# The first cross attention's 160 keys as 128 + 32 in place of 80 + 80, and a weight centring moved from GpSimd to VectorE in pieces

## What is computed

```python
q = (layernorm(x) @ Wq + bq)      # 16 batches, 64 queries, 16 heads of 16
k = (ctx_1024 @ Wk + bk)          # 1024 keys, most of them masked
v = (ctx_1024 @ Wv + bv)
scores = where(mask, q @ k.T / 4, -1e9)
x = x + softmax(scores) @ v @ Wo + bo
...
q = layernorm_per_head(layernorm(x) @ L0_attn_Wq.T)   # 16 heads of 64; k likewise
```

## Time and profile before

| | |
|---|---|
| time before, median of 3 runs | 843.26 us (841.45 to 844.18) |
| span of the profiled execution | 844.3 us; no separate time is given for it |
| PE / PEld busy | 684.7 us (81%) / 525.9 us (62%) |
| DVE / ACT / POOL busy | 421.2 / 328.4 / 144.2 us |
| iterations b = 1 to 15 of the first cross attention | 44.36 to 201.14 us |

### The profile page before, as it was taken

The page is one execution under the profiler, slowest core; times in us unless marked ns, Lnnn a source line. Parts: engine busy times, 40 slices in busy tenths (PEclk is TensorE's granted clock), DMA queues, the critical chain, the costliest instruction groups (busy, mean ns, idle before and its releaser), DMA issues. The chain is left out here.

```text
span 844.3 us, 18960 instructions
## 1 busy us (share of the span) xinstructions
PE 684.7 (81%) x7638; PEld 525.9 (62%) x7638; DVE 421.2 (50%) x907; ACT 328.4 (39%) x881; POOL 144.2 (17%) x213
## 2 busy tenths in 40 slices
PE   3778887789899999995787689989986764278996
PEld 2556665565456666663665546579985643178995
DVE  5436787764545445514587275836657344011111
ACT  1235444443445544442577363331224141132332
POOL 1011112201100000003334232091000211211121
PEclk9879998999999999995889699989998965598999
DMA  6920000001900000004000000000000009791110
GB/s 174 357 65 2 2 2 1 1 1 34 230 2 2 1 2 1 2 1 127 2 2 3 1 0 2 2 2 2 0 2 2 0 4 318 274 368 39 46 51 23
DMA packets 33161, 45.30 MB, mean 54 GB/s; under 512 B 7998, under 2 KB 26175, under 8 KB 32960
## 3 DMA queue, kind: packets, MB, share of 16 engines
q1 hardware_dynamic: 28672, 33.31, 12.3%
q0 software_dynamic: 2256, 7.37, 2.7%
q10 hardware_dynamic: 2160, 3.60, 1.6%
HBM read 36.91 MB, written 7.89 MB: 53 GB/s over the span
## 5 line engine op out<-in xcount | busy, mean ns | idle before, releaser
L393 ACT ACTIVATE a_pr<-a_bank,a_nms 128x160 f32<-128x160 f32 x128 | 49.1, 391 | 59.4 <-DVE a_nms L723 57.0
L859 PE MATMUL a_bank<-ident,a_pr 128*80 128x128 f32 x256 | 41.5, 289 | 25.7 <-DVE a_pt L699 23.2
L2101 ACT ACTIVATE f_hb<-f_bank,cols 128x128 f32<-128x128 f32 x96 | 35.2, 367 | 63.1 <-PE f_bank L2219 58.2
L859 PEld LDWEIGHTS a_bank<-ident,a_pr 128*80 128x80 f32 x256 | 26.1, 124 | 46.3 <-ACT a_pr L393 31.8
L2219 PE MATMUL f_bank<-f_xts,f_w 128*128 x384 | 51.6, 293 | 0.8 <-DVE f_xts L2171 0.8
L2219 PEld LDWEIGHTS f_bank<-f_xts,f_w 128*128 128x128 f32 x384 | 50.2, 208 | 1.7 <-issue 1.2
L629 DVE TENSOR_REDUCE a_negmx<-a_bank 128x2 f32<-128x320 f32 x64 | 30.4, 475 | 33.6 <-PE a_bank L851 33.6
L699 DVE COPY a_pt<-a_bank 80x512 f32<-80x512 f32 x60 | 40.9, 682 | 10.5 <-PE a_bank L859 9.8
L2229 PE MATMUL f_bank<-f_w,f_hb 128*128 128x256 f32 x192 | 44.0, 383 | 0.0
L2229 PEld LDWEIGHTS f_bank<-f_w,f_hb 128*128 128x128 f32 x192 | 36.2, 194 | 4.5
L358 POOL TENSOR_TENSOR a_spr<-a_linv,a_hm 128x128 f32<-128x128 f32 x32 | 12.1, 400 | 148.9 <-DVE a_linv L678 136.3
(11 more groups left out here) (361 smaller groups left out, 1607.2 us busy)
## 6 DMA issues: line engine op xcount, KB each, us to landing
f_w<-in_f_w SPq DMA_DIRECT2D x16, 1024.0 KB, 9.8
slots<-a_zero POOLq DMA_DIRECT2D x1, 4112.0 KB, 18.7
f_xs<-slots ACTq DMA_DIRECT2D x13, 257.0 KB, 2.7
...
rows<-in_rows SPq DMA_DIRECT2D x1, 2120.0 KB, 10.1
...
```

The source lines that it names most:

```text
L393: i = act.activation(pr[:, p, j, k, :], s_bank[j][:, k * KW:(k + 1) * KW], ACT.Exp, bias=nms[:, p, j, k:k + 1], accum_out=rsum[:, p, 2 * j ...
L859: m = pe.transpose(dst[0:HK, (2 * k + a) * P:(2 * k + a + 1) * P], pr[:, p, j, k, a * HK:(a + 1) * HK], c.ident[:, :])
L2101: act.activation(hb[:, m, :], bank[m % 4][:, 0:P], ACT.Gelu, bias=c.col("f_b1", e * FC + m)).then_inc(z["act"], 1)
```

## The change

Keys 0 to 127 of the window are now one full part, and keys 128 to 159 a tail. Values: one product of 128 keys, and the tail's values in four column tiles of 32 so that the tail of j lies on partitions 32 j (`tail_values`, L846). Turns: three per batch in place of four: turn 0 (j = 0, 1) and turn 1 (j = 2, 3) of four transposes each, and turn 2 with the tails of all j, eight products with the identity in tiles of 32 columns (L873); they are copied as 512, 512 and 256 columns. Weigh: for each k, four products over the 128 keys (L881) and four over the 32 in tiles of 32 x 32 (L885). The tail values stand behind turn 1, and turn 2 stands behind keys. The centring is in eight pieces (four per weight), each a sum, a scaling and an addition over 512 elements on DVE, at the end of iterations 6 to 13; making the weights `wt` binary moves from iteration 10 to 14. At the start, the product behind `actq` goes to `k_bank`, DVE reads it before the second half of its statistics, and PE waits for it before the keys, not before the queries.

The core of the diff, with the general loop's part left out:

```diff
@@ -196,9 +196,9 @@
-        vs = sb("vs", [HK, 2, 2, D])
+        vs = sb("vs", [P, 2, D + S])
...
-        pt = sb("pt", [HK, 4, 512])
+        pt = sb("pt", [P, 2 * KW // 32, P])
@@ -373,12 +373,6 @@
             for b in range(NT + 1, B):
-                if b in (10, 12):
-                    i, wx = (b - 10) // 2, (bwq, bwk)[(b - 10) // 2]
-                    pool.wait_ge(U["wmean"], i + 1)
-                    tv = wx[:, :, :].rearrange("p k (h n) -> p (k h) n", n=DA)
-                    pool.tensor_tensor(tv, tv, wm[:, i, :].unsqueeze(2).to_broadcast([P, KC * HA, DA]),
-                                       ALU.add).then_inc(U["wcent"], 1)
                 spread(b)
...
@@ -603,18 +597,18 @@

+            dve.wait_ge(z["actp"], 1)
+            dve.tensor_scalar(actq[:, :], k_bank[:, 0:S], HD ** -0.5, None, ALU.mult).then_inc(z["actq"], 1)
+            dve.wait_ge(s_ident, 64)
+            dve.wait_ge(z["actq"], 1)
+            for e in range(2):
+                dve.tensor_scalar(acte[:, e, :], actq[:, :], c.eo[:, e:e + 1], None, ALU.mult).then_inc(z["acte"], 1)
             dve.wait_ge(s_x[1], 16)
...
                 normed(A0, xn, t, 2)
-            dve.wait_ge(z["actp"], 1)
-            dve.tensor_scalar(actq[:, :], o_bank[:, 0:S], HD ** -0.5, None, ALU.mult).then_inc(z["actq"], 1)
-            dve.wait_ge(s_ident, 64)
-            dve.wait_ge(z["actq"], 1)
-            for e in range(2):
-                dve.tensor_scalar(acte[:, e, :], actq[:, :], c.eo[:, e:e + 1], None, ALU.mult).then_inc(z["acte"], 1)
             dve.wait_ge(z["acte"], 2)
@@ -624,6 +618,10 @@
                         ).then_inc(z[f"qbd{e}"], 1)
+
+            def turned_out(g, src, done):
+                a, n = 4 * g, 4 if g < 2 else 2
+                dve.tensor_copy(pt[:, a:a + n, :].rearrange("p a n -> p (a n)"), src[:, 0:n * P]).then_inc(done, 1)

...
@@ -694,9 +692,9 @@
-            def turned(b, j):
-                dve.wait_ge(T["tp"], 4 * (b - 1) + j + 1)
-                dve.tensor_copy(pt[:, j, :], t_bank[0:HK, :]).then_inc(T["pt"], 1)
+            def turned(b, g):
+                dve.wait_ge(T["tp"], 3 * (b - 1) + g + 1)
+                turned_out(g, t_bank, T["pt"])
@@ -705,20 +703,22 @@
-            def center(i):
-
-                if i == 0:
-                    dve.wait_ge(s_bw, 64)
-                dve.reduce_sum(wm[:, i, :], (bwq, bwk)[i][:, :, :].rearrange("p k (h n) -> p (k h) n", n=DA), AXX).then_inc(U["wsum"], 1)
-                dve.wait_ge(U["wsum"], i + 1)
-                dve.tensor_scalar(wm[:, i, :], wm[:, i, :], -1.0 / DA, None, ALU.mult).then_inc(U["wmean"], 1)
+            def center(i, part):
+                n = 4 * i + part
+                wp = (bwq, bwk)[i][:, :, :].rearrange("p k (h n) -> p (k h) n", n=DA)[:, 8 * part:8 * part + 8, :]
+                mp = wm[:, i, 8 * part:8 * part + 8]
+                dve.reduce_sum(mp, wp, AXX).then_inc(U["wsum"], 1)
+                dve.wait_ge(U["wsum"], n + 1)
+                dve.tensor_scalar(mp, mp, -1.0 / DA, None, ALU.mult).then_inc(U["wmean"], 1)
+                dve.wait_ge(U["wmean"], n + 1)
+                dve.tensor_tensor(wp, wp, mp.unsqueeze(2).to_broadcast([P, 8, DA]), ALU.add).then_inc(U["wcent"], 1)
...
-                    if b > 1 and j:
-                        turned(b - 1, j - 1)
+                    if b > 1 and j % 2:
+                        turned(b - 1, j // 2)
@@ -726,22 +726,24 @@
-                    turned(b - 1, 3)
+                    turned(b - 1, 2)
...
-                if b in (6, 8):
-                    center((b - 6) // 2)
-                if b == 10:
+                if 5 < b < 14:
+                    if b == 6:
+                        dve.wait_ge(s_bw, 64)
+                    center((b - 6) // 4, (b - 6) % 4)
+                if b == 14:
...
-            for j in range(4):
-                turned(B - 1, j)
-                if j == 0:
+            for g in range(3):
+                turned(B - 1, g)
+                if g == 0:
@@ -809,7 +811,7 @@
             pe.wait_ge(z["const"], CONST_ANYB)
-            pe.matmul(o_bank[:, 0:S], anyb[0:S, :], c.ident[0:S, 0:S], start=True, stop=True).then_inc(z["actp"], 1)
+            pe.matmul(k_bank[:, 0:S], anyb[0:S, :], c.ident[0:S, 0:S], start=True, stop=True).then_inc(z["actp"], 1)

@@ -834,11 +836,17 @@
-            def values(src, a):
+            def values(src):
...
-                    m = pe.matmul(v_bank[0:HK, a * D:(a + 1) * D], src[:, kk, a * HK:(a + 1) * HK], wv[:, kk, :],
-                                  start=(kk == 0), stop=(kk == KC - 1))
-                return m
+                    pe.matmul(v_bank[:, 0:D], src[:, kk, 0:KM], wv[:, kk, :], start=(kk == 0), stop=(kk == KC - 1))
+
+            def tail_values(src, done):
+                for kk in range(KC):
+                    for j in range(4):
+                        m = pe.matmul(v_bank[32 * j:32 * j + 32, D:D + S], src[:, kk, KM:KW],
+                                      wv[:, kk, :].rearrange("p (k j f) -> p j k f", k=KC, j=4)[:, j, :, :],
+                                      start=(kk == 0), stop=(kk == KC - 1), tile_position=(0, 32 * j), skip_group_check=True)
+                m.then_inc(done, 1)
@@ -853,30 +861,38 @@
-            def turn(p, j, done, dst):
-                for k in range(KC):
-                    for a in range(2):
-                        m = pe.transpose(dst[0:HK, (2 * k + a) * P:(2 * k + a + 1) * P],
-                                         pr[:, p, j, k, a * HK:(a + 1) * HK], c.ident[:, :])
+            def turn(p, g, done, dst):
+                if g < 2:
+                    for jj in range(2):
+                        for k in range(KC):
+                            m = pe.transpose(dst[:, (2 * jj + k) * P:(2 * jj + k + 1) * P], pr[:, p, 2 * g + jj, k, 0:KM],
+                                             c.ident[:, :])
+                else:
+                    for k in range(KC):
+                        for j in range(4):
+                            m = pe.matmul(dst[32 * j:32 * j + 32, k * P:(k + 1) * P], pr[:, p, j, k, KM:KW], c.ident[:, :],
+                                          start=True, stop=True, tile_position=(0, 32 * j), skip_group_check=True)
...
-                    for a in range(2):
-                        for j in range(4):
-                            f = k * P + 32 * j
-                            m = pe.matmul(o_bank[32 * j:32 * j + 32, k * P:(k + 1) * P], vs[:, p, a, f:f + 32],
-                                          pt[:, j, (2 * k + a) * P:(2 * k + a + 1) * P], start=(a == 0), stop=(a == 1),
-                                          tile_position=(0, 32 * j), skip_group_check=True)
-                            if k == KC - 1 and a == 1:
-                                m.then_inc(done, 1)
+                    for j in range(4):
+                        f = k * P + 32 * j
+                        pe.matmul(o_bank[32 * j:32 * j + 32, k * P:(k + 1) * P], vs[:, p, f:f + 32], pt[:, 2 * j + k, :],
+                                  start=True, stop=False, tile_position=(0, 32 * j), skip_group_check=True)
+                    for j in range(4):
+                        jr = slice(32 * j, 32 * j + 32)
+                        m = pe.matmul(o_bank[jr, k * P:(k + 1) * P], vs[jr, p, D + 32 * k:D + 32 * k + 32], pt[jr, 8 + k, :],
+                                      start=False, stop=True, tile_position=(32 * j, 32 * j), skip_group_check=True)
+                        if k == KC - 1:
+                            m.then_inc(done, 1)
...
-            pe.wait_ge(z["actq"], 1)
...
+            pe.wait_ge(z["actq"], 1)
...
@@ -931,15 +946,15 @@
-            def turn_b(b, j):
-                pe.wait_ge(T["probs"], 4 * (b - 1) + j + 1)
-                if j:
-                    pe.wait_ge(T["pt"], 4 * (b - 1) + j)
-                turn(b % 2, j, T["tp"], t_bank)
+            def turn_b(b, g):
+                pe.wait_ge(T["probs"], 4 * (b - 1) + min(4, 2 * g + 2))
+                if g:
+                    pe.wait_ge(T["pt"], 3 * (b - 1) + g)
+                turn(b % 2, g, T["tp"], t_bank)
...
-                pe.wait_ge(T["pt"], 4 * b)
+                pe.wait_ge(T["pt"], 3 * b)
@@ -962,9 +977,8 @@
-                    for a in range(2):
-                        m = values(ct[:, 1, :, :], a)
-                    m.then_inc(T["v"], 1)
+                    values(ct[:, 1, :, :])
+                    tail_values(ct[:, 1, :, :], T["v"])
@@ -978,15 +992,16 @@
-                    values(ct[:, b, :, :], 0)
+                    values(ct[:, b, :, :])
...
-                    values(ct[:, b, :, :], 1).then_inc(T["v"], 1)
-                    turn_b(b - 1, 2)
-                    turn_b(b - 1, 3)
+                    tail_values(ct[:, b, :, :], T["v"])
...
+                if b > 1:
+                    turn_b(b - 1, 2)
+                if b < B - 1:
@@ -1006,7 +1021,7 @@

-            pe.wait_ge(U["wcent"], 2)
+            pe.wait_ge(U["wcent"], 8)
```

(4 more changed lines are left out.)

24 lines of the change are left out of this document (10 added, 14 removed).

## The result

The changed kernel takes **815.35 us** (median; before, on the same chip, 842.36): 0.967 of before, 95% interval 0.962 to 0.972, or 27.0 us less. The forecast was 816.5. The profiled execution has a span of 815.1 us, before 844.3.

A forecast was written before the change was run, and what follows sets the result against it. The cycle was taken as scores, DVE's chain up to the third copy, then a full queue on PE. Terms -3.9 - 14.3 - 0.4 - 10.1 + 2.0 = -26.7 off 843.26 gave 816.5 us; range 809 to 829.

The forecast's parts named there:

- Start, -3.9: At the kernel's start, PE's queries begin at about 12.45 us and not 16.38, without the wait for `actq`: -3.9 us.
- Thirteen iterations, -1.1 each: In iterations b = 2 to 14, the distance between scores falls from 9.19 to 8.09 us: -14.3 in all.
- masks wait for ACT alone, with 0.3 us to spare on PE: In each iteration, ACT's exponentials end 5.55 us behind scores, later than PE's queue reaches masks at 5.23.
- b = 1, nothing; end, -0.4: The general loop and b = 1 gain in values what weigh loses, 0; iteration 15 and the turns behind it: -0.4 us.
- The stalls, -10.1: In the loop, two iterations of 14.81 and 13.66 us lose their stalls behind GpSimd's centring: together -10.1 us.
- Odd pieces, +2.0: Centring pieces in iterations 7, 9, 11 and 13 make DVE late for the next maximum: 0.5 x 4 = +2.0 us.
- What stands behind moves as a block: The six stages behind the loop hang on PE, with no load late, and move together.
- B: Rival: changes of tile shape on PE are free, weigh takes 1.01 us, cycle 7.58: 811 us; chance 0.20.
- C: Rival: a change of tile shape costs twice, 0.34 us, weigh 2.03, cycle 8.62: 822 to 829 us; chance 0.21.
- D: Rival: shape changes make the kernel slower than before; decides at 0.68 us each, 852 us at 0.8; chance 0.05.
- E: Rival: DVE's `nms` waits for GpSimd's `spread` and the addition behind it, PE's turn 1 wait stays: 823 us; chance 0.02.
- the granted clock would fall with a thinner PE: Named way to fail: PE's granted clock falls because its work got thinner; no size given.

The follow-up runs named there:

- a1: The kernel before with only the start of the change (PE's wait moved from the queries to the keys): 840.40 us, ratio 0.9955 to before.
- b1: The change with weigh grouped, both full rows then both tail rows, one shape change inside; sums leave out the first half's full products: 812.74 us, ratio 0.9640 to before.
- b5: The change with weigh mirrored (full, tail, tail, full), two shape changes inside it and not three: 813.41 us, ratio 0.9680 to before.
- a2: The kernel before with only the centring of the change, eight pieces on DVE: 835.84 us, ratio 0.9919 to before.
- a3: The kernel before with only the split of the keys, centring on GpSimd and start as before: 823.12 us, ratio 0.9763 to before.
- b3: The change with the odd centring piece ahead of the addition that waits for project: 813.80 us, ratio 0.9671 to before.
- b4: The change with the eight centring additions of 512 elements on GpSimd, sums and scalings on DVE: 814.25 us, ratio 0.9677 to before.
- c0: The change itself, unaltered, timed again beside other kernels: 814.02 us, ratio 0.9658 to before.
- c2: The change with each row of weigh cut into halves of 64 columns on all four tiles, seven shape changes: 823.18 us, ratio 0.9785 to before.

## Why the prediction was right, point by point

- *Start, -3.9:* right, -3.75 in the trace and -3.8 alone (a1).
- *Thirteen iterations, -1.1 each:* the mechanism was right in the main: turn 1 waits for the first copy, and weigh and its changes of shape stand behind masks. That masks wait for ACT alone, with 0.3 us to spare on PE, is not borne out. I had counted the change of shape once for each row of small tiles, on its way out, so five in a cycle; there are seven, and those on the way in show: turn 1, ahead of the tail values, is 0.12 longer than forecast, and keys, ahead of turn 2, 0.19. PE's queue so comes to masks at 5.47 and not 5.23, and ACT at 5.42 and not 5.55. That the two still meet near the forecast is luck. The cycle fell by 1.26 and not 1.10: masks 0.08 earlier, weigh 0.10 shorter, since a change of shape in weigh costs 0.13 to 0.15 (b1, b5) and not 0.17. 13 x 1.26 = -16.4 and not -14.3: this term is mis-sized by 2.1.
- *b = 1, nothing; end, -0.4:* b = 1 fell from 11.13 to 10.37 (-0.76), b = 2 by 0.2 more than the cycle, iteration 15 from 9.09 to 8.49 (-0.6). I had put the longer weigh against the shorter values and turns and called it even; it is not. (Iterations 1 and 2 together take 21.4 to 21.8 us in before, a1 and a2, and 19.1 to 19.9 in after, a3, b3, b4 and c0.)
- *The stalls, -10.1:* right. a2 shows it alone, and that the odd pieces then cost 0.84 each; a3 keeps the stalls and pays 8.1 for them.
- *Odd pieces, +2.0:* +0.43 x 4 = +1.7, for the reason given; b3 takes it away by moving the piece.
- *What stands behind moves as a block:* right at most places within 0.8 us from 205 us of before to 770 of after. It is off by 1.6 us behind the first product with a lower clock, by 1.2 to 3.6 in one later stretch of 55 us and 1.5 in another, and by 3.8 at a DMA wait in the last stage; the code there is the same in both kernels. The reason given, that the stages hang on PE and no load is late, was a wrong reading: in before PE waits 20.97 us for the load `f_xs<-slots` where the last stage begins and 10.3 more for the later ones, and 8.44 and 9.19 us for DVE in the stages ahead of it. Those waits moved along with the rest because the work that they wait for stands behind the loop too.

The terms as measured give -3.8 - 16.4 - 0.8 - 0.2 - 0.6 - 10.1 + 1.7 = -30.2, the -30.16 of the loop's end; forecast were -26.7. The medians of whole executions say -27.0 and -28.4. So the forecast hit the median more closely than its own terms deserve: the loop gained 3.5 us more than forecast, and the code behind the loop varies by 7 us from trace to trace (637.9 to 645.1). That the median came out within 1.2 us of the forecast is in part luck; the parts of the loop are the better test, and they hold as listed.

Rivals: B (a change of shape is free) and C and D (it costs 0.34 or more) fall to b1, b5 and c2, at 0.13 to 0.15 each; E to the `nms` rows of after, none of which takes more than 0.16 us from b = 3 on. That the granted clock would fall with a thinner PE was a risk named: it is 1.00 over the loop from b = 3 to its end.
